# Heads rotated as rows on GpSimd, and a mixture's last tiles mixed inside the next attention

## The reference

```
x = _layernorm(x + _L0_xattn_ref(x, ctx, ctx, q_norm_w, k_norm_w, proj_w, proj_b))   # "L0x"
x = _layernorm(x + _L0_ffn_ref(x, router_weight, w1, w2))                            # "L0f"
x = _layernorm(x + _L1_attn_ref(x, Wq, Wk, Wv, Wo))                                  # "L1a"
```

## Time and profile before

| | |
|---|---|
| three runs | 4296.24, 4301.33 (median), 4304.2 us |
| profiled execution | 4300.37 us, span 4298.6 us |
| L0x, from its first copy of `ctx` to its last row | 344.6 to 698.1 |
| L0f, to its last side work | 698.4 to 1146.3 |
| L1a, from its weights to its last row | 1147.3 to 1697.5 |

### The profile page before, as it was taken

The page is one execution under the profiler, slowest core; times in us unless marked ns, Lnnn a source line. Parts: engine busy times, 40 slices in busy tenths (PEclk is TensorE's granted clock), DMA queues, the critical chain, the costliest instruction groups (busy, mean ns, idle before and its releaser), DMA issues. The chain is left out here.

```text
span 4298.6 us, 137640 instructions
## 1 busy us (share of the span) xinstructions
PE 3699.6 (86%) x48696; PEld 2734.9 (64%) x48696; DVE 3249.1 (76%) x7860; ACT 2228.5 (52%) x4080; POOL 1616.4 (38%) x2677
## 2 busy tenths in 40 slices
PE   8997998688299998998996858998989687879986
PEld 6775677466177776776776636776764344457764
DVE  7996887344488887887995187997977577769975
ACT  4664553345244443666882445666864354535553
POOL 4663343665411111112454442332223244435544
PEclk9998997899599999999996988999999788989988
DMA  2011112587200000110001840000112000000001
GB/s 78 27 48 38 37 37 62 167 248 188 66 2 0 0 0 11 43 43 28 18 16 58 248 139 13 14 14 30 33 38 64 21 1 0 0 19 24 24 14 39
DMA packets 293808, 209.64 MB, mean 49 GB/s; under 512 B 51137, under 2 KB 272193, under 8 KB 293441
## 3 DMA queue, kind: packets, MB, share of 16 engines
q1 hardware_dynamic: 233760, 157.72, 12.8%
q0 software_dynamic: 12288, 25.19, 2.0%
q10 hardware_dynamic: 47520, 23.60, 1.8%
HBM read 122.49 MB, written 54.53 MB: 41 GB/s over the span
## 5 line engine op out<-in xcount | busy, mean ns | idle before, releaser
L1355 DVE TENSOR_TENSOR L0f_G<-L0f_SG,L0f_psH 128x512 f32<-128x512 f32 x106 | 73.0, 689 | 170.5 <-ACT L0f_SG L1099 127.8
L2224 POOL TENSOR_TENSOR L1a_rs<-L1a_ag,eps 128x1 f32<-128x1 f32 x64 | 12.1, 189 | 476.3 <-DVE L1a_ag L2384 476.3
L938 POOL DMA_INDIRECT L0f_sorted_x<-X,L0f_IDX x128 | 123.1, 961 | 94.1 <-DMA L0f_sorted_x<-X,L0f_IDX 35.7
L959 POOL DMA_INDIRECT L0f_YG<-L0f_sorted_y,L0f_IDY x128 | 124.4, 972 | 69.8 <-issue 35.9
L2311 PE MATMUL L1a_psO<-L1a_WO,L1a_OT 128*64 128x128 f32 x2048 | 125.9, 276 | 6.7 <-ACT L1a_OT L2335 5.7
L2245 PE MATMUL L1a_psF<-L1a_XT,L1a_WQ 128*128 128x256 f32 x512 | 130.8, 389 | 0.5 <-DVE L1a_KT L2200 0.5
L2311 PEld LDWEIGHTS L1a_psO<-L1a_WO,L1a_OT 128*64 128x64 f32 x2048 | 110.6, 137 | 25.2 <-ACT L1a_OT L2335 23.6
L1915 PE MATMUL L3a_psH<-L3a_UT,L3a_WG 128*128 128x512 f32 x128 | 80.9, 718 | 50.1 <-DVE L3a_G L2028 48.6
L1033 PEld LDWEIGHTS L0f_psO<-L0f_WB,L0f_G 128*128 128x128 f32 x848 | 102.9, 192 | 25.5 <-issue 25.5
L586 ACT ACTIVATE L3x_PT<-L3x_psP 128x512 f32<-128x512 f32 x128 | 69.6, 595 | 88.5 <-PE L3x_psP L521 88.5
L586 ACT ACTIVATE L0x_PT<-L0x_psP 128x512 f32<-128x512 f32 x128 | 69.5, 595 | 83.1 <-PE L0x_psP L521 83.1
(11 more groups left out here) (684 smaller groups left out, 12996.0 us busy)
## 6 DMA issues: line engine op xcount, KB each, us to landing
L0f_WB<-in_w12a SPq DMA_DIRECT2D x53, 312.0 KB, 3.5
L0f_XB<-L0f_sorted_x SPq DMA_DIRECT2D x53, 256.0 KB, 4.0
L0f_sorted_y<-L0f_YB ACTq DMA_DIRECT2D x53, 256.0 KB
L1m_WB<-in_w12b SPq DMA_DIRECT2D x37, 321.0 KB, 4.0
L1m_XB<-L1m_sorted_x SPq DMA_DIRECT2D x37, 256.0 KB, 3.8
L1m_sorted_y<-L1m_YB ACTq DMA_DIRECT2D x37, 256.0 KB
L0f_sorted_x<-L0f_AC SPq DMA_DIRECT2D x27, 256.0 KB, 4.0
L1m_sorted_x<-L1m_AC SPq DMA_DIRECT2D x27, 256.0 KB, 3.6
```

The lines of the kernel that those rows point to most:

```text
L938: nc.gpsimd.indirect_dma_start(out=sorted_x[p][:, :], out_offset=bass.IndirectOffsetOnAxis(ap=IDX[:, k, t:t + 1], axis=0), in_=X[:, t, :], ...
L959: nc.gpsimd.indirect_dma_start(out=YG[:, b % 4, k, t % TB, :], out_offset=None, in_=sorted_y[p][:, :], in_offset=bass.IndirectOffsetOnAxis ...
L1355: nc.vector.tensor_tensor(G[0:f, J % 2, c, :], SG[0:f, c, :], up, ALU.mult).then_inc(S["g_ready"].sem, 1)
```

## The change

Two edits, and what they need.

**L0x by rows.** The rotation is made before the turn, on rows, by GpSimd alone: `rope_rows`, ten instructions a pair. For `X` and for `ctx` each: the rows times a table of weight and cosine (128x256), the swapped rows times weight and sine (two instructions of 128x128, every second element), the sum (128x256), and the multiplication with the root's reciprocal, which also writes the heads in the order of the attention (so its writes go in steps of four elements). The tables are `turn_rows`, made by VectorE in `head_roots` from 128x256 of new `angles` and four new rows of weights (14 instead of 10 rows in `row`), fetched at L0a's end. TensorE turns the pair of `ctx` and of `X` into one bank (four transposes), ScalarE copies all 512 columns at once into QK. The products with IQ and SWAP, `rope_parts`, the adds into KT and QT, the copies CT and XT, and the value matmuls are gone; the values are fetched as rows of `ctx` (VS, two DMAs a pair) and copied to VB by ScalarE. L0x gets `late` = 1.

**L0f's last 24 tiles.** `HERE` = 10: only batches 0 to 9 are gathered and mixed in L0f, at steps of 2 blocks in the last part (42, 44, ..., 52). All sixteen side works lie inside the blocks: at J = 16, 18, 20, 22, 24, 28, 31, 34 to 41 and 43, each with its rows fetched one block ahead (before: two). The weights of L1a are fetched by SyncE at the end of L0f. In L1a, `LateRows` gathers tile 40+j in slot j-3 (two gathers on GpSimd), mixes it in slot j (VectorE, behind the slot's own work), takes its statistics in j+1, its root in j+2 and j+3, and writes its rows in j+4 (ScalarE). The first 32 tiles of L1a are written out.

```diff
+                        if by_rows and N.ok:
+                            made(sp, "o_v", N.p - 1)
+                            for a in range(2):
+                                pace(sp, S)
+                                sp.dma_start(VS[64 * a:64 * a + 64, N.u, :, :], io["ctx"][bass.ds(N.p * 256, 256), :].rearrange("(s k) d -> k s d", s=4)).then_inc(parity_sem("ctx_in", N), 16)
...
+                    def rope_rows(N):
+                        pair = lambda ap: ap.rearrange("p (t d) -> p t d", t=2)
+                        table = lambda n: tables[:, n, :].unsqueeze(1).to_broadcast([P, 2, D])
+                        both = (CS[:, N.u], X[:, bass.ds(N.t, 2), :])
+                        parity_wait(g, "rows_in", N, 16)
+                        made(g, "ctx_normed", N.p)
+                        made(g, "xs", N.p)
+                        pace(g, S)
+                        for n, rows in ((1, both[1]), (0, both[0])):
+                            nc.gpsimd.tensor_tensor(pair(RA[:, n, 0]), rows, table(2 - 2 * n), ALU.mult).then_inc(S["rope_parts"].sem, 1)
+                            for k in range(2):
+                                m = nc.gpsimd.tensor_tensor(pair(RA[:, n, 1])[:, :, k:D:2], rows[:, :, 1 - k:D:2], table(3 - 2 * n)[:, :, k:D:2], ALU.mult)
+                            m.then_inc(S["rope_parts"].sem, 1)
+                        for n in (1, 0):
+                            made(g, "rope_parts", 4 * N.p + 4 - 2 * n)
+                            nc.gpsimd.tensor_tensor(RA[:, n, 0], RA[:, n, 0], RA[:, n, 1], ALU.add).then_inc(S["rope_sums"].sem, 1)
+                        made(g, "f_k", N.p - 1)
+                        for n, dst, st, done in ((1, XS, stat, "xs"), (0, CN, stat2, "ctx_normed")):
+                            made(g, "rope_sums", 2 * N.p + 2 - n)
+                            pace(g, S)
+                            r = st[:, bass.ds(N.t, 2), :].rearrange("p t (r b) -> p (t r) b", b=HQ).unsqueeze(3).to_broadcast([P, 8, HQ, HD])
+                            nc.gpsimd.tensor_tensor(dst[:, N.u].rearrange("p t (r d b) -> p (t r) b d", r=4, b=HQ),
+                                                    RA[:, n, 0].rearrange("p (g b d) -> p g b d", g=8, d=HD), r, ALU.mult).then_inc(S[done].sem, 1)
...
+                    def fill_rows(N):
+                        made(pe, "xs", N.p + 1)
+                        made(pe, "ctx_normed", N.p + 1)
+                        made(pe, "o_k", N.p)
+                        for n, rows in enumerate((CN, XS)):
+                            for a in range(2):
+                                m = nc.tensor.transpose(psF[:, (2 * n + a) * P:(2 * n + a + 1) * P], rows[:, N.u, a, :], ident)
+                        m.then_inc(S["f_k"].sem, 1)
...
+                        if T.par == 0 and N.ok and by_rows:
+                            made(act, "f_k", N.p + 1)
+                            made(act, "scores", 2 * N.p - 2)
+                            parity_wait(act, "keys_in", N - 4, 16 * HQ)
+                            nc.scalar.activation(QK[:, N.u].rearrange("p c t -> p (c t)"), psF[:, :], ACT.Copy).then_inc(S["o_k"].sem, 1)
...
-                    at += 2.5 if gated else 2
-            SIDES = NBATCH // 2
+                    at += (2.5 if p == 1 else 2) if gated else 2
+            free = [J for J in range(first[1] + 1, BLOCKS) if J not in step_after]
+            side_after = dict(zip(free[0:14:2] + free[14:], range(NBATCH))) if gated else {}
...
+                        if J + 1 in side_after:
+                            side_rows(side_after[J + 1])
+                    if later is not None:
+                        later.load_weights(sp)
...
+            def fetch(self, g, T):
+                j = self.tile(T, -3)
...
+                self.made(g, "mix", j - 3)
+                for k in range(2):
+                    nc.gpsimd.indirect_dma_start(out=self.YG[:, j % 4, k, :], out_offset=None, in_=self.sorted_y[t >= self.edge][:, :],
+                                                 in_offset=bass.IndirectOffsetOnAxis(ap=self.IDY[:, k, t:t + 1], axis=0)).then_inc(S[f"gathered{j % 4}"].sem, 16)
...
+            def mix(self, dv, T):
+                j, a, b = self.tile(T, 0), self.tile(T, 1), self.tile(T, 3)
...
+                    nc.vector.scalar_tensor_tensor(self.ACC[:, j % 4, :], self.YG[:, j % 4, 0, :], self.gate[:, 0, t:t + 1], X[:, t, :], ALU.mult, ALU.add).then_inc(S["own"].sem, 1)
...
+                    nc.vector.bn_aggr(self.ag[:, a % 4, :], self.st[:, a % 2, :]).then_inc(S["in_stats"].sem, 1)
...
+                    nc.vector.scalar_tensor_tensor(self.ACC[:, j % 4, :], self.YG[:, j % 4, 1, :], self.gate[:, 1, t:t + 1], self.ACC[:, j % 4, :], ALU.mult, ALU.add).then_inc(S["mix"].sem, 1)
...
+                    nc.vector.scalar_tensor_tensor(self.nb[:, b % 4:b % 4 + 1], self.ag[:, b % 4, 0:1], -1.0, self.rt[:, b % 4, 1:2], ALU.mult, ALU.mult).then_inc(S["late_shift"].sem, 1)
...
+                    nc.vector.bn_stats(self.st[:, j % 2, :], self.ACC[:, j % 4, :]).then_inc(S["in_bn"].sem, 1)
...
+                        later.root(g, T)
+                        later.fetch(g, T)
+                    pipeline(g, slot, 3, LATE_FIRST)
```

More of the change, by code:

```diff
@@ L20 @@
 FIRST_W, FIRST_X, MORE_X = 10, 16, 8
+LATER, LATE_FIRST = 24, 32
 LN_EPS = 1e-5
@@ L112, in p, with pipeline @@
         return self.c // 2 if self.i is None else self.i * 2 + self.c // 2
-def pipeline(eng, slot, ahead=3):
-    first, turns = 8, 13
+def pipeline(eng, slot, ahead=3, first=8):
+    turns = (60 - first) // 4
     for c in range(-ahead, first):
@@ L257, in attention @@
             late = 1 if ks is None and not keymask else 0
-            turn_c = cross and norm is not None
-            raw = cross and norm != "ln"
+            by_rows = tables is not None
+            turn_c = cross and norm is not None and not by_rows
+            raw = cross and norm != "ln" and not by_rows
             zero = zeros[:, 0:1]
@@ L499, in slot @@
                         N = T + 2
-                        if T.par == 0 and N.ok:
+                        if T.par == 0 and N.ok and by_rows:
+                            fill_rows(N)
+                        if T.par == 0 and N.ok and not by_rows:
                             made(pe, "o_tx", N.p + 1)
@@ L505, in slot @@
                         K = T + 1
-                        if T.par == 1 and K.ok:
+                        if T.par == 1 and K.ok and not by_rows:
                             made(pe, "o_v", K.p)
@@ L756, in _ @@
                         nc.scalar.activation(st[:, :, :], st[:, :, :], ACT.Sqrt)
+                @block.vector
+                def _(dv):
+                    for n, (part, weight) in enumerate(((0, "qn"), (1, "qns"), (0, "kn"), (1, "kns"))):
+                        nc.vector.tensor_tensor(turn_rows[:, n, :], angles[:, part, :], R(weight), ALU.mult)
         TB = BATCH // P
@@ L924, in _ @@
                             expert(J + 3)
-                        if gated and p == 1 and k % 2 == 0 and k // 2 < SIDES:
-                            side_rows(k // 2)
-                    if gated:
-                        for b in range(SIDES, NBATCH):
-                            side_rows(b)
+                        if J + 1 in side_after:
+                            side_rows(side_after[J + 1])
+                    if later is not None:
+                        later.load_weights(sp)
                 @block.gpsimd
@@ L1355, in _ @@
                                 nc.vector.tensor_tensor(G[0:f, J % 2, c, :], SG[0:f, c, :], up, ALU.mult).then_inc(S["g_ready"].sem, 1)
-                            k = J - first[1] - 2
-                            if k >= 0 and k % 2 == 0 and k // 2 < SIDES:
-                                side_work(k // 2)
+                            if J in side_after:
+                                side_work(side_after[J])
                         else:
@@ L2213, in slot @@
                         N, A = T + 2, T - 2
+                        later.all_rows(g, T)
                         if T.par == 0 and N.ok:
@@ L2336, in slot @@
                         copies(act, T, 2)
-                    pipeline(act, slot, 2)
+                        later.rows(act, T)
+                    pipeline(act, slot, 2, LATE_FIRST)
                 @block.vector
@@ L2342, in slot @@
                         A, E = T - 1, T - 2
+                        later.all_rows(dv, T)
                         if T.ok:
@@ L2384, in slot @@
                             nc.vector.bn_aggr(ag[:, A.par, :], st[:, A.par, :]).then_inc(S["stats"].sem, 1)
-                    pipeline(dv, slot, 2)
+                        later.mix(dv, T)
+                    pipeline(dv, slot, 2, LATE_FIRST)
             S.advance(dict.fromkeys(("scores", "maxed", "shifted", "probs", "turned_a", "turned_b", "pt_a", "pt_b", "pv", "normed",
                                      "ot_a", "ot_b", "proj", "res", "bn", "stats", "var_eps", "rstd", "out_rows", "summed", "recip"), TILES))
```

(13 more changed lines are left out.)

173 lines of the change are left out of this document (126 added, 47 removed).

## The result

The changed kernel takes 4206.69 us (median of 4 runs, 4201.27 to 4210.09) against 4301.24 for the kernel before on the same chip: ratio 0.978, 95% interval 0.9763 to 0.9797, 95 us faster. The forecast was 4171, the range 4148 to 4215. The profiled execution took 4203.98 us, its span 4202.2 (before 4298.6), so the span holds 96.4 of it.

What follows compares the result with a forecast made beforehand. The prediction took TensorE and VectorE as nearly full in L0x and L1a, with TensorE idle behind L0f's last block. Sum: 4300.37 - 62 (L0x) - 77 (L0f's tail) + 10 (L1a) = 4171 us, range 4148 to 4215.

Steps and rivals of the forecast that it cites:

- L0x's pair, 8.2 forecast: L0x: GpSimd 7.63 us a pair, just ahead of VectorE; imperfect overlap makes 8.2 instead of 10.17, gaining 62 us.
- SyncE has two DMAs more a pair and one fewer; DMA share is 0.12 here, hidden: L0x: SyncE's changed transfers were taken to cost nothing in the 8.2 us pair.
- E: L0x: rotation was hidden anyway, pair stays near 10.17 us through another wait (key DMAs or ctx rows); 4233, chance 0.04.
- The tail, 77 forecast: End of L0f: gathers pace the last steps, L1a's first copy comes at 1079.5 against 1156.76; gain 77 us (60 to 80).
- so this is hidden behind the gathers: L0f: blocks end some 4 us later, at no cost, as batch 9 can't be mixed before 1067.5.
- and 1 us for the barrier: L0f to L1a: work ends near 1074.5, then 1 us is allowed before L1a's block starts.
- rival B: L0f's blocks starve on side DMAs, or VectorE's L1a slot is 9.04 us; costs 11 to 25, 4182 to 4196, chance 0.10.
- L1a, 10 forecast: L1a: late rows lengthen VectorE's tile to 8.6 us against 8.16, losing 10 us over 24 tiles (0 to 21).
- Rival A: L0x: stepped access is dear on GpSimd, pair 8.8 to 10 us, gain 5 to 43; 4190 to 4228, chance 0.20.
- Rival D: L0x: GpSimd's last multiplications take 2.9 us each instead of 0.63, pair 12.3; from there the kernel is slower; chance 0.03.
- C: All goes better: L0x's pair 7.6 us, L1a's late rows nearly free; 4144 and up to 4155, chance 0.10.
- its own signs: L0x: L662 4.1 us apart, GpSimd above 90%, last multiplications 0.63, clock 1.00; L1a: first copy near 1018, tiles 8.6 apart.

## Why the prediction came out 36 us low

The range held the result; the single number did not, and in three places.

1. **L0x's pair, 8.2 forecast, 8.83 measured: 20 us.** The engines' work was sized well, as the run with the ctx rows first shows: VectorE 95.67% of 7.91 is 7.57 (forecast 7.44, with small waits 7.6). GpSimd is busy 91.53% of 7.91, 7.24 (forecast 7.63): its single durations are above the forecast, but successive ones overlap by some ns in the record. The step that failed is "SyncE has two DMAs more a pair and one fewer; DMA share is 0.12 here, hidden". The share was right and beside the point: what counts is when the transfer is asked for. The cause stood among the rivals, as E ("the rows of `ctx` that SyncE fetches only behind the copy of two pairs before"), with 0.04 and priced as all or nothing. GpSimd waited 1.34 us a pair. The run with the ctx rows first shows the cause: one transfer moved in SyncE's queue gives 30 us, 0.92 a pair, more than the 20 that were missing. For the prediction had 8.2 for two engines so close, and without the wait the pair is 7.91: 0.3 a pair too much there hid a third of what was left out, by luck. Part of the 30 is TensorE's clock. The prediction had named its fall under what would make it wrong; it fell in places, to a mean of 0.74 from 480 to 500, and with the wait gone it was back at 1.00. It did not make TensorE the bound. What lets it fall stays open: TensorE's share of 450 to 550 is the same with the falls and without (85.20 and 85.62).

2. **The tail, 77 forecast, 68 measured: 9 us.** The stage's work ended nearly on time: from its first transfer ScalarE's last row ended after 1035.8-656.4 = 379.4 us, where the sum (1076.5 less 1 us for the barrier) has 377.1. But it did not get there as foreseen. VectorE waited 7.7 us in all for YG, less than foreseen. The blocks' last copy of YB came 373.4 into the stage against 363.9 before, 9.5 later and not 4, and "so this is hidden behind the gathers" failed: ScalarE's rows of batches 7 to 9 stand behind that copy, and GpSimd's last root behind the first of these rows. In the profiled execution of the changed kernel the statistics of batch 9 were ready at the same time (VectorE's last instruction for them ended at 1032.35, the root started at 1032.62); in the runs with the ctx rows first the blocks alone set the end. That the sum came within 2.3 us of it is luck. Why the blocks are 9.5 later stays open. What failed in the price is the term "and 1 us for the barrier": GpSimd's DRAIN takes 10.28 us here and holds the core 7.4. It was 3.7 us in the kernel before and all but hidden, and no row of it was looked at. The run with the root moved shows the gap closing while the DRAIN keeps its length. (The last step of the sum is off by itself: 1076.5 and 2.5 us of gathers are 1079.0, not 1079.5.) Of rival B, the side rows were indeed late, 29.5 us of VectorE's waits, up to 3.2 each; the two runs that took these waits away show no gain in time that can be told.

3. **L1a, 10 forecast, 14 measured: 4 us.** The late rows cost 10.7 us, as sized. The other 3.6 are the DRAIN again, 4.585 against 0.662; it comes with L1a's 48 gathers, for with 32 slots written out and no gathers it stayed 0.662. No term stood for it.

20 + 9 + 4 = 33, and the profiled execution took 4203.98 us against 4171; the median lies 3 above it.

**Rival A** (stepped access dear) named the right neighbourhood, 4190 to 4228, by the wrong mechanism. The halves cost 516 and not 730, the last multiplications 669 and not 1260: 0.3 us a pair in all. The Trainium skill, "GPSIMD Engine Reference", section 7, gives half as much again for reads whose inner step is above 8 bytes. By it, extended to these writes, they would have taken 940 ns (an estimate from that rule and L334's 628); the rows have 664 and 669, so the rule doesn't carry over to these writes that step by 16 bytes. **Rival D** needed 2.9 us for the same instruction and is out. **C** (pair 7.6) fell with the wait; without it the pair is 7.91. On the shared interfaces the prediction went by one instruction beside gathers, and added nothing. The write back of X takes 340 ns without the rotation and 580 beside its products. It cost at most the 0.2 us a pair that came back without the rotation, 6 us of the stage. The Trainium skill, "GPSIMD Engine Reference", section 1, names VectorE's instructions in a mode with two ports beside those with two SBUF inputs; the write back would fit that, though no run here shows in which mode it runs.

**By its own signs**: the last multiplication at 0.67 and L1a's loss came as foreseen. GpSimd above 90% and the clock at 1.00 did not, and came with the moved transfer. L0x_ON was 4.4 apart instead of 4.1, and L1a's first copy at 1046.4 instead of 1018 (20 of it from L0x).

What stays open: whether GpSimd's DRAIN really begins its count anew at 128 gathers; what makes L0f's blocks end 9.5 us later; what lets the clock fall in L0x; and whether 28 late tiles are better than 24. Nobody tried the smallest change for the ctx rows either: in GpSimd's stream, the wait for them behind the products of X, which don't read them.

## What to carry to other kernels

- When work moves to another engine, follow its inputs too: for each transfer that it now waits for, find what stands ahead of the request in the issuing queue. A share of 0.12 of the DMA engines says nothing about that. Ask for a buffer's next rows when the buffer is free, not behind a wait that belongs to something else.
- At a boundary between blocks read the drains of all engines. One that is all but hidden today (3.7 us) is on the path (10.3 us, 7.4 of them with nothing beside it) when the count of gathers changes. Here it was hidden again when that engine's last dependent step went to another one.
- A long wait in the list is not a cost until something behind it moves: 30 us of waits for the side rows could be removed with no gain that could be told, and 1.34 us a pair for the ctx rows was worth 30 us of the kernel.
- At the end of a stage follow each engine's written order, and not only the data: ScalarE's rows of a batch that had long been mixed stood behind the last block's copy, and another engine's last step waited for them.
